# A routed expert kernel: four payload buffers, the last group's scatters among the tiles, and two thirds of the word loads on SyncE's queue

## The chip, the cores and the metric

The kernel runs on one core of a Trainium2 chip. The metric is device microseconds of one execution, and the median of the runs counts. A core has TensorE (PE), VectorE (DVE), ScalarE (ACT), GpSimd (POOL) and SyncE (SP); each works through its own instructions in order and waits on semaphores. SP, ACT and POOL also issue DMA transfers. In the profile an issue on SP or ACT stands as SPq or ACTq, a DMA issued by POOL as POOL.

## What is computed

There are 16 x 256 tokens of width 128 and 16 contexts of 64 keys.

```
x = x + attention(keys and values from ctx, queries from layernorm(x))
n = layernorm(x)
probs, idx = top_k(softmax(n @ Wr + br), 2)        # 8 experts, 2 for each token, probs normed to sum 1
h = layernorm(relu(n @ W1[e] + b1[e])) * g1[e] + be1[e]
y = layernorm(relu(h @ W2[e] + b2[e])) * g2[e] + be2[e]
x = x + sum over the 2 chosen experts of prob * y
```

Everything is float32. The kernel computes only the chosen experts' rows: 8192 token rows, sorted by expert into tiles of 128.

## The kernel before

**Group stage.** The 4096 tokens are 32 tiles in 8 groups of 4. For each group the kernel does attention, the second layernorm, the router and the choice of two experts. It counts, per expert, where each token's row goes (`pos`, a row number in the DRAM array `slot_rows`). A group's rows are put into a payload buffer `pay`: 128 high and 128 low halves in float16, then two words, the row number to which the answer must go, and the gate (L1202 `pay_hi` on ACT, L1556 `pay_lo` and L1741 `gate_rows` on DVE). There are two payload buffers, taken in turn; whoever writes a buffer waits until the eight scatters of the group two earlier have landed. SP copies the rows for the second choice (L533). POOL then sends eight indirect DMAs a group, one for each choice and tile (L659 `payload_out`), which scatter 128 rows each.

**Tile stage.** 71 tiles of 128 slot rows go through the experts. SP fetches a tile's rows transposed (L513 `tile_rows`, eleven buffers; it reads the row numbers from the table `row_tab` into registers, eight at a time). PE computes up and down products (`up`, `down_hi`, `down_lo`), ACT and DVE do ReLU, layernorms and the gate in a software pipeline: at position p ACT does the gate product of tile p-4 (L1378 `gate_share`, tile `rg`), which needs the two words of each row, and the final scaling (L1389, buffers `z`, five in turn). POOL loads the two words of every row of a tile (L686 `words`, `words_of`, 1 KB, twelve buffers) and scatters the finished rows into the DRAM array `answers` (L677 `answer`). In POOL's order, position p has the answer of tile p-4, then the words of tile p+2.

The first 24 tiles (`WHOLE`) hold only rows of the first four groups, so SP starts their transpositions during the last group; before tile 24, SP and POOL wait for all scatters. SP sends eleven transpositions, then the last group's payload copy, then eight stores of zero rows behind the experts' last rows (L571), then the other tiles. Of the last group's eight scatters POOL issues the first four ahead of the words and the other four at positions 2, 5, 8 and 11.

**End.** When the answers of a group are complete, SP fetches them (L551 `answers_back`, spread over the later tiles). PE adds the offset terms (L1071 `offset_sums`), DVE adds the two answers (L1957 `with_first`, L1967 `with_second`), ACT and SP store.

Of the kernel before, what the change touches and what calls it, by code (L numbers as in the profile page):

```python
# [23 lines left out]
def build(nc, A, out):  # L24
    P = 128
# [28 lines left out]
    ROW = 2 * D + 4  # L54
    MANTISSA, BIAS, LN2 = 23, 127, 0.6931471805599453
# [6 lines left out]
    with ctx:  # L62
# [125 lines left out]
        pos = sb("pos", [P, 2, K, GT], U32)  # L188
        pay = [sb(f"pay{n}", [P, K, GT, ROW], F16) for n in range(2)]
# [31 lines left out]
        NW, NS, LEAD = 12, 8, 2  # L221
# [122 lines left out]
        def as_row(ap, n):  # L344
# [3 lines left out]
        ld_wkq, ld_wv, ld_wo, ld_bq, ld_bvo, ld_br, ld_b1, ld_gb, ld_b2, ld_g2, ld_be2 = (  # L348
            signal("ld_" + n) for n in (
                "wkq", "wv", "wo", "bq", "bvo", "br", "b1", "gb", "b2", "g2", "be2"))  # L350
# [15 lines left out]
        p_setup, c_setup, c_exp, c_wrc, c_wkq, s_var1, s_guess1, s_sd, s_sel = (signal(n) for n in (  # L366
            "pe_setup", "act_setup", "exp_loaded", "wr_centred", "wkq_centred", "var1_eps", "rstd1_guess", "sd1",
# [8 lines left out]
        def ends(sem, order, step, done, ins):  # L376
# [12 lines left out]
        s_copy = [signal(f"pay_copy{n}") for n in range(2)]  # L389
        s_sc = [signal(f"scatter{n}") for n in range(2)]  # L390
# [6 lines left out]
        s_diag, s_share, p_share, s_shareT, p_off = (signal(n) for n in (  # L397
            "be2_diag", "shares", "pe_shares", "sharesT", "pe_offsets"))


        s_gm, s_ss, s_ss3, p_tot, s_tot, s_scale, s_w1x = (signal(n) for n in (
            "gains", "square_sums", "gain_square", "pe_totals", "totals", "scale", "w1_less_last"))
# [18 lines left out]
        s_word = [signal(f"words{n}") for n in range(NS)]  # L421
        s_backs = [signal(f"back{n}") for n in range(3)]
# [5 lines left out]
        def scattered(n):  # L428

            return 16 * K * GT * (n // 2 + 1)  # L430
# [39 lines left out]
        def sync(eng):  # L470
# [19 lines left out]
            eng.dma_start(b2row[:, :], flat("L0_ffn_b2").rearrange("(o n) -> o n", o=1)).then_inc(ld_b2, 16)  # L490
            eng.wait_ge(s_diag, 1)
# [19 lines left out]
            rows = []  # L511

            def tile_rows(j):  # L513
                if j >= NX:
                    eng.wait_ge(p_h, j - NX + 1)
                if j % E == 0:
                    half_regs = regs[j // E % 2 * E:(j // E % 2 + 1) * E]
                    table = row_tab[:, 0:WHOLE] if j < WHOLE else row_tab[:, :]
                    rows[:] = rows_of(half_regs, table, j, 0, E * REGION + (SPARE - 1) * P)
                here = bass.ds(rows[j % E], P)  # L520
                eng.dma_start_transpose(xsT[j % NX], slots[here, 0:2 * D]).then_inc(s_row[j % NX], 16)

            for g in range(GROUPS):
                if g == GROUPS - 1:
# [3 lines left out]
                    for n in range(2):  # L528
                        eng.wait_ge(s_sc[n], scattered(AHEAD - 2 + n))
# [3 lines left out]
                eng.dma_start(pay[g % 2][:, 1, :, 0:2 * D], pay[g % 2][:, 0, :, 0:2 * D]).then_inc(s_copy[g % 2], 16)  # L533
# [10 lines left out]
                for h in range(2):  # L544
# [4 lines left out]
                              ).then_inc(ld_g2, 16)  # L549
# [15 lines left out]
            for j in range(NX, SLOT_TILES):  # L565
# [6 lines left out]
                if j == WHOLE:  # L572
                    eng.wait_ge(s_zero, 16 * (E + 1))
                    for n in range(2):
                        eng.wait_ge(s_sc[n], scattered(GROUPS - 2 + n))
# [16 lines left out]
        def gpsimd(eng):  # L592
# [9 lines left out]
            eng.memset(be2_diag[:, :], 0.0).then_inc(s_diag, 1)  # L602
            eng.memset(zero_rows[:, :, :], 0.0).then_inc(s_zeros, 1)
            for n in range(2):
# [54 lines left out]
            def payload_out(g, k, i):  # L659
# [5 lines left out]
                if i == 0 and k == 1:  # L665
                    eng.wait_ge(s_copy[g % 2], 16 * (g // 2 + 1))
                eng.indirect_dma_start(  # L667
                    slot_words, bass.IndirectOffsetOnAxis(ap=pos[:, g % 2, k, i:i + 1], axis=0),
                    pay[g % 2][:, k, i, :].bitcast(U32), None).then_inc(s_sc[g % 2], 16)
# [16 lines left out]
            def words(j):  # L686

                if j == 0:
                    eng.wait_ge(s_tab, 1)
                    for n in range(2):  # L690
                        eng.wait_ge(s_sc[n], scattered(AHEAD - 2 + n))
                if j == WHOLE:
                    eng.wait_ge(s_tab, 2)
                    eng.wait_ge(s_zero, 16 * (E + 1))
                    for n in range(2):
                        eng.wait_ge(s_sc[n], scattered(GROUPS - 2 + n))
                if j % E == 0:
                    half_regs = regs[j // E % 2 * E:(j // E % 2 + 1) * E]
                    table = row_tab[0:1, 0:WHOLE] if j < WHOLE else row_tab[0:1, :]
# [17 lines left out]

        @block.tensor
        def tensor(eng):
# [131 lines left out]
            def gains():  # L851
                eng.wait_ge(ld_gb, 32)
# [4 lines left out]
            def totals():  # L857
                eng.wait_ge(s_ss, 2 * FC)
                eng.wait_ge(s_ss3, 1)
# [3 lines left out]
            def w_rows(h, part):  # L863

                first = h * H * FC
                if part == 0:
                    eng.wait_ge(ld_b2, 16)
# [53 lines left out]
            eng.wait_ge(c_wrc, 1)  # L921
            eng.wait_ge(ld_wo, 16)
            ends(p_setup, PE_SETUP, "wo", done, mm(bank[6][:, 0:D + E], WO, ident_wr[:, :]))
            eng.wait_ge(c_wkq, 1)
# [6 lines left out]
            eng.wait_ge(ld_wv, 16)  # L931
            mm(bank[7][:, 0:D + E], WV, woT[:, :])
            eng.wait_ge(ld_bvo, 32)
# [186 lines left out]
        def scalar(eng):  # L1120
# [81 lines left out]
            def pay_hi(g):  # L1202
                eng.wait_ge(s_xt, g + 1)
                if g >= 2:
                    eng.wait_ge(s_sc[g % 2], scattered(g - 2))
                if g == 0:
                    eng.wait_ge(s_const, 1)
                copy(pay[g % 2][:, 0, :, 0:D - 1], xt[:, :, 0:D - 1]).then_inc(s_hi, 1)
                copy(pay[g % 2][:, :, :, 2 * D:2 * D + 2].bitcast(U32)[:, :, :, 0],
# [21 lines left out]
            def c2_scaled():  # L1231
                eng.wait_ge(ld_off, 32)
# [23 lines left out]
            eng.dma_start(bcol[:, 1:2], A["L0_xattn_bv"].rearrange("(p o) -> p o", o=1)).then_inc(ld_bvo, 16)  # L1256
            eng.dma_start(bcol[:, 2:3], A["L0_xattn_bo"].rearrange("(p o) -> p o", o=1)).then_inc(ld_bvo, 16)
            eng.dma_start(brow[:, :], row1("L0_ffn_br").to_broadcast([P, E])).then_inc(ld_br, 16)
            eng.wait_ge(s_ones, 2)
            eng.activation(prob[0:1, 0, 0:1], ones[0:1, 0:1], ACT.Exp).then_inc(c_exp, 1)  # L1260
# [163 lines left out]
        def vector(eng):  # L1424
# [3 lines left out]
            def wkq_centred():  # L1428
# [3 lines left out]
                                         op0=ALU.mult, op1=ALU.add).then_inc(c_wrc, 1)  # L1432
# [123 lines left out]
            def pay_lo(g):  # L1556
                p = pay[g % 2]
# [37 lines left out]
            def pos_(g):  # L1595
                eng.wait_ge(q_pos, poss.n)
                if g >= 2:
                    eng.wait_ge(s_sc[g % 2], scattered(g - 2))
                with nc.allow_low_precision(reason="one whole number under 2 ** 24 among zeros"):
                    eng.tensor_reduce(pos[:, g % 2, :, :], pick[:, :, :].rearrange("p k (i e) -> p k i e", i=GT), AX.X,  # L1600
# [421 lines left out]
```

## Time and profile before

| | us |
|---|---|
| median of 3 runs | 272.37 |
| lowest and highest run | 269.18, 274.11 |
| profiled execution: span from first to last instruction | 268.4 |
| what lies around the span | not in the profile; the lowest run is 0.8 above the span, the median 4.0 |
| mean granted TensorE clock in the profiled execution | 0.955 |

The span is one execution; the run times are of others, so a sum made against the span is carried to the median by their difference. Times in rows are microseconds from the span's start. In a row of the timeline the first number is the start, the second the length; a group that is shown merged has its count at the end.

### The profile page before, as it was taken

To read this page: it belongs to the slowest core of one execution; us is meant where nothing else is said; L and a number is where in the kernel's file an instruction comes from. 1 tells how busy PE (TensorE), PEld (TensorE's weight loads), DVE (VectorE), ACT (ScalarE), POOL (GpSimd) and SP (SyncE) were. 2 spreads that over 40 slices of the span, in tenths; PEclk is the share of its full clock that TensorE was granted. 3 is DMA by queue.
4 is the path that set the end of the run, shared out by engine and by line. 5 is a ranking of instruction groups with operands and counts; after the bars stand their busy time and mean duration, and the time that the engine had idled before them with its cause. 6 is when DMAs were issued, how large, how long until landed. Compare 5 with 4: busy or idle time off the path is not lost.

```text
span 268.4 us, 10286 instructions
## 1 busy us (share of the span) xinstructions
PE 239.9 (89%) x2960; PEld 194.0 (72%) x2960; DVE 229.7 (86%) x1091; ACT 211.5 (79%) x795; POOL 190.6 (71%) x300
## 2 busy tenths in 40 slices
PE   1989779899888677679899999999999999999994
PEld 1564567777666434579899979999999999999330
DVE  0667986867689989689999988999999999999875
ACT  2465675789888888757999988999999999999700
POOL 8602277877757777775888888888888888878640
PEclk9997995899999759999999999999999999999999
DMA  6998398123425234354333443333315686772257
GB/s 159 313 299 295 91 271 279 51 89 92 139 82 136 83 91 99 84 119 94 84 90 67 89 82 81 73 72 75 84 33 142 155 155 141 149 143 86 68 187 233
DMA packets 48676, 34.56 MB, mean 129 GB/s; under 512 B 26871, under 2 KB 42743, under 8 KB 48620
## 3 DMA queue, kind: packets, MB, share of 16 engines
q1 hardware_dynamic: 38972, 22.80, 32.8%
q0 software_dynamic: 6592, 9.00, 12.7%
q10 hardware_dynamic: 3056, 2.11, 2.6%
q8 instruction: 25, 0.41, 0.7%
q14 instruction: 31, 0.25, 0.3%
HBM read 15.11 MB, written 12.02 MB: 101 GB/s over the span
## 4 chain that ended last, share of the span: by engine, by line
DVE 37%; issue 22%; PE 20%; ACT 9%; DMA 5%; DVEq 4%; SPq 1%; ACTq 0%
PE bank L721 15%; DVE vo L1873 8%; PE bank L725 4%; DMA w2f<-in_L_ffn_W 3%; DVE rs L1914 3%; DVE cx L1903 3%; DVE kq L1866 3%; DVE w2f L1653 3%; DVEq L1880 2%; DVE st L1891 2%; ACT ex L1175 2%; DVE mv L1897 1%; DMA wr<-in_L_ffn_Wr 1%; ACT xt L1198 1%; DVE topi L1573 1%
## 5 line engine op out<-in xcount | busy, mean ns | idle before, releaser
L679 POOL DMA_INDIRECT answers<-vo,words_of x71 | 70.6, 994 | 23.8 <-issue 19.4
L667 POOL DMA_INDIRECT slot_rows<-pay,pos x64 | 65.5, 1023 | 27.9 <-issue 18.5
L721 PE MATMUL bank<-kb_room,w1h 128*128 128x128 f16 x568 | 55.2, 219 | 1.7 <-issue 1.7
L725 PE MATMUL bank<-w2h,rh 128*128 x284 | 51.4, 219 | 1.6 <-ACT w2l L1122 1.6
L725 PE MATMUL bank<-rh 128*128 128x129 f16 x284 | 51.5, 220 | 0.0
L725 PE MATMUL bank<-w2l,rh 128*128 x284 | 51.4, 219 | 0.0
L721 PE MATMUL bank<-kb_room,w1l 128*128 128x128 f16 x284 | 51.2, 219 | 0.0
L1866 DVE SCALAR_TENSOR_TENSOR kq<-bank,rh 128x512 f16<-128x512 f32 x71 | 47.8, 673 | 0.1
L721 PEld LDWEIGHTS bank<-kb_room,w1h 128*128 x568 | 43.6, 98 | 2.6 <-issue 2.6
L1347 ACT ACTIVATE rh<-bank 128x512 f16<-128x512 f32 x71 | 41.1, 579 | 5.2 <-PE bank L721 4.2
L705 POOL DMA_DIRECT2D words_of<-slot_rows x71 | 40.8, 576 | 2.0 <-issue 1.8
L725 PE MATMUL bank<-w2h,kq 128*128 x284 | 40.3, 222 | 2.1 <-DVE kq L1866 1.7
L725 PE MATMUL bank<-rh,kq 128*128 128x129 f16 x284 | 39.8, 221 | 0.0
L1873 DVE CUSTOM_DVE_ANT_0 vo<-bank,square_mask 128x257 f32<-128x257 f32 x71 | 29.6, 418 | 2.2 <-issue 1.2
L725 PEld LDWEIGHTS bank<-w2h,kq 128*128 128x128 f16 x284 | 26.2, 97 | 6.6 <-DVE kq L1866 3.6
L725 PEld LDWEIGHTS bank<-w2h,rh 128*128 128x128 f16 x284 | 27.8, 98 | 3.4 <-ACT w2l L1122 1.8
L725 PEld LDWEIGHTS bank<-rh,kq 128*128 128x128 f16 x284 | 27.9, 98 | 0.0
L725 PEld LDWEIGHTS bank<-w2l,rh 128*128 128x128 f16 x284 | 27.8, 98 | 0.0
L721 PEld LDWEIGHTS bank<-kb_room,w1l 128*128 x284 | 27.8, 98 | 0.0
L725 PEld LDWEIGHTS bank<-rh 128*128 128x128 f16 x284 | 27.8, 98 | 0.0
L1389 ACT ACTIVATE vo<-cx,rg 128x128 f32<-128x128 f32 x71 | 27.5, 388 | 0.1
L1886 DVE SCALAR_TENSOR_TENSOR cxT<-bank,rs,c 128x128 f32<-128x128 f32 x71 | 24.9, 351 | 0.2
(259 smaller groups left out, 601.7 us busy)
## 6 DMA issues: line engine op xcount, KB each, us to landing
x_tok<-in_x SPq DMA_DIRECT2D x8, 256.0 KB, 7.7
w1f<-in_L_ffn_W SPq DMA_DIRECT2D x2, 1024.0 KB, 8.8
pay<-pay SPq DMA_DIRECT2D x8, 256.0 KB, 3.3
w1f<-answers SPq DMA_DIRECT2D x8, 256.0 KB
w2f<-answers SPq DMA_DIRECT2D x8, 256.0 KB, 2.9
kb_room<-slot_rows SPq DMA_TRANSPOSE x71, 3.3
words_of<-slot_rows POOLq DMA_DIRECT2D x71, 1.0 KB
answers<-vo,words_of POOLq DMA_INDIRECT x71
```

The source lines that it names most:

```text
L667: eng.indirect_dma_start(slot_words, bass.IndirectOffsetOnAxis(ap=pos[:, g % 2, k, i:i + 1], axis=0), pay[g % 2][:, k, i, :].bitcast(U32), ...
L679: eng.indirect_dma_start(answers, bass.IndirectOffsetOnAxis(ap=words_of[:, j % NW, 0:1], axis=0), z[j % NZ], None).then_inc(s_ans[j % NZ], 16)
L705: eng.dma_start(words_of[:, j % NW, :], slot_words[bass.ds(rows[j % E], P), D:]).then_inc(s_word[j % NS], 16)
L721: return eng.matmul(dst, lhsT, rhs, start=start, stop=stop)
L725: return eng.matmul(dst, lhsT, rhs, start=start, stop=False, skip_group_check=True)
L1347: eng.activation(rh_all(j), psH[j % 3][:, :].rearrange("p (c n) -> p c n", c=FC), ACT.Relu).then_inc(s_rh, 1)
L1389: eng.activation(z[j % NZ], w_[j % 3], ACT.Copy, scale=rg[j % 4][:, :]).then_inc(s_z, 1)
L1653: t = eng.scalar_tensor_tensor(out=w2f[:, n, :], in0=w2f[:, n, :], scalar=g1c[:, n:n + 1], in1=w2_mean[:, e_ * D:(e_ + 1) * D], op0=ALU.mu ...
L1866: eng.scalar_tensor_tensor(out=rl[j % 2][:, :, :], in0=psH[j % 3][:, :].rearrange("p (c n) -> p c n", c=FC), scalar=0.0, in1=rh_all(j), op ...
L1873: eng.tensor_tensor_reduce(squares[:, :], psY[j % 3][:, D:D + 2 * P + 1], square_mask[j % 2][:, :], 1.0, 0.0, ALU.mult, ALU.add, s2[j % 4] ...
L1886: eng.scalar_tensor_tensor(out=u[j % 3], in0=psY[j % 3][:, 0:D], scalar=rs1(j), in1=c2[:, bass.ds(off[j], D)], op0=ALU.mult, op1=ALU.add). ...
L1903: eng.scalar_tensor_tensor(out=w_[j % 3], in0=ur[j % 3], scalar=mv2[j % 4][:, 0:1], in1=g2[:, bass.ds(off[j], D)], op0=ALU.subtract, op1=A ...
```

## The change

The payload and position buffers are four instead of two, and a writer waits for the scatters of four groups earlier. All eight scatters of the last group go at the even positions 0 to 14 of POOL's tile order. Words of the tiles below `WHOLE`, and of odd tiles after it, are loaded by SP, each behind the transposition eight tiles ahead of it; POOL keeps the even tiles from 24. Besides, some setup semaphores are joined, the row of b2 is loaded earlier, and `b2row` and `w2_rows` share the room of other arrays.

```
+    NP = 4
...
-        b2row = sb("b2row", [1, E * D])
-        w2_rows = sb("w2_rows", [2, E * D])
+        b2row, w2_rows = w2_mean[0:1, :], c2[0:2, :]
...
-        pay = [sb(f"pay{n}", [P, K, GT, ROW], F16) for n in range(2)]
+        pos = sb("pos", [P, NP, K, GT], U32)
+        pay = [sb(f"pay{n}", [P, K, GT, ROW], F16) for n in range(NP)]
...
-        NW, NS, LEAD = 12, 8, 2
+        NW, NS, NSG, LEAD = 12, 8, 3, 2
+        WORDS_BEHIND = E
...
+        def words_by_sp(j):
+            return j < WHOLE or j % 2 == 1
+        def word_at(j):
+            return (j if j < WHOLE else WHOLE + (j - WHOLE) // 2) if words_by_sp(j) else (j - WHOLE) // 2
...
 SP:
+            eng.dma_start(b2row[:, :], flat("L0_ffn_b2").rearrange("(o n) -> o n", o=1)).then_inc(ld_gb, 16)
...
+            def words(j):
+                if words_by_sp(j):
+                    if j >= NW:
+                        eng.wait_ge(s_ans[(j - NW) % NZ], answered(j - NW))
+                    n = word_at(j)
+                    if n >= NS:
+                        eng.wait_ge(s_rg, tile_of_word(n - NS) + 1)
+                    eng.dma_start(words_of[:, j % NW, :], slot_words[bass.ds(place_of[j], P), D:]
+                                  ).then_inc(s_word[n % NS], 16)
...
                     for j in range(NX):
                         tile_rows(j)
+                        if j >= WORDS_BEHIND:
+                            words(j - WORDS_BEHIND)
...
                 tile_rows(j)
+                words(j - WORDS_BEHIND)
                 if j in back_at:
                     answers_back(back_at[j])
+            for j in range(SLOT_TILES - WORDS_BEHIND, SLOT_TILES):
+                words(j)
...
 POOL:
-            for g in range(GROUPS):
+            for g in range(GROUPS - 1):
                 for k in range(K):
                     for i in range(GT):
-                        if g < GROUPS - 1 or k == 0:
-                            payload_out(g, k, i)
+                        payload_out(g, k, i)
+            last_out = [(GROUPS - 1, k, i) for k in range(K) for i in range(GT)]
...
-                eng.dma_start(words_of[:, j % NW, :], slot_words[bass.ds(rows[j % E], P), D:]).then_inc(s_word[j % NS], 16)
-            for j in range(LEAD):
-                words(j)
+                n = word_at(j)
+                if n >= NSG:
+                    eng.wait_ge(s_rg, j - 2 * NSG + 1)
+                eng.dma_start(words_of[:, j % NW, :], slot_words[bass.ds(rows[j % E], P), D:]
+                              ).then_inc(s_word_even[n % NSG], 16)
             for p in range(SLOT_TILES + 4):
                 if 0 <= p - 4 < SLOT_TILES:
                     answer(p - 4)
-                if p + LEAD < SLOT_TILES:
+                if p + LEAD < SLOT_TILES and not words_by_sp(p + LEAD):
                     words(p + LEAD)
-                if p % 3 == 2 and p // 3 < GT:
-                    payload_out(GROUPS - 1, 1, p // 3)
+                if p % 2 == 0 and p // 2 < K * GT:
+                    payload_out(*last_out[p // 2])
...
 ACT:
-                eng.wait_ge(s_word[j % NS], 16 * (j // NS + 1))
+                eng.wait_ge(*word_landed(j))
```

## Rows read from the trace of the kernel before

**Rows 1.** The page's first part: busy us, share of the span, instructions.

```profile
PE 239.9 (89%) x2960; PEld 194.0 (72%) x2960; DVE 229.7 (86%) x1091; ACT 211.5 (79%) x795; POOL 190.6 (71%) x300
```

**Rows 2.** Stretch: length, busy PE, PEld, DVE, ACT, POOL, clock, DMA share, GB/s.

```profile
196.00:206.00 10.00, 10.00 (x175) 9.65 (x173) 10.00 (x45) 9.84 (x44) 8.18 (x12) 1.00 0.40 107
```

**Rows 3.** Timeline of VectorE (three sums of squares) and TensorE, tile stage.

```profile
118.76 0.42 DVE L1873 CUSTOM_DVE_ANT_0 vo<-bank,square_mask 128x257 f32<-128x257 f32 x1
...
179.96 0.42 DVE L1873 CUSTOM_DVE_ANT_0 vo<-bank,square_mask 128x257 f32<-128x257 f32 x1
181.81 0.42 DVE L1873 CUSTOM_DVE_ANT_0 vo<-bank,square_mask 128x257 f32<-128x257 f32 x1
...
113.48 0.22 PE L725 MATMUL bank<-w2h,rh 128*128 x1
115.28 0.22 PE L725 MATMUL bank<-w2h,rh 128*128 x1
```

**Rows 4.** Timeline of GpSimd; landing of its answers; ScalarE's products 10 and 13.

```profile
181.70 0.98 POOL L679 DMA_INDIRECT answers<-vo,words_of  x1 [0.30 <-issue]
182.68 0.57 POOL L705 DMA_DIRECT2D words_of<-slot_rows  x1
...
142.18 0.96 POOL L679 DMA_INDIRECT answers<-vo,words_of  x1 [0.30 <-issue]
...
DMA to landing us min/median/max: 2.8/2.9/3.3
...
142.43 0.40 ACT L1389 ACTIVATE vo<-cx,rg 128x128 f32<-128x128 f32 x1
148.06 0.39 ACT L1389 ACTIVATE vo<-cx,rg 128x128 f32<-128x128 f32 x1
```

**Rows 5.** The end: the chain of waits, then timelines of ACT, POOL and SP.

```profile
249.34 15.23 PE bank L721 x30
...
254.68 0.40 ACT L1389 ACTIVATE vo<-cx,rg 128x128 f32<-128x128 f32 x1
...
256.96 1.50 POOL L679 DMA_INDIRECT answers<-vo,words_of  x1 [0.30 <-issue]
...
260.56 0.90 SPq L557 DMA_DIRECT2D w2f<-answers  x2
```

**Rows 6.** Timeline of payload and scatter; landing of rows stored to and transposed from `slot_rows`.

```profile
104.03 0.63 ACT L1122 ACTIVATE pay<-xt 128x508 f16<-128x508 f32 x1
...
97.13 0.96 POOL L667 DMA_INDIRECT slot_rows<-pay,pos  x1 [0.30 <-issue]
...
DMA to landing us min/median/max: 2.7/3.3/4.8
```

**Rows 7.** Timeline of VectorE: the second part of the row table.

```profile
116.43 0.18 DVE L1700 SCALAR_TENSOR_TENSOR row_tab<-bank,slot_at 1x47 uint32<-1x47 f32 x1
```

**Rows 8.** Timeline of SP's queue: zero rows, then tiles 15, 16 and 23.

```profile
117.86 4.02 SPq L571 DMA_DIRECT2D slot_rows<-zero_rows  x8
...
128.80 1.17 SPq L521 DMA_TRANSPOSE kb_room<-slot_rows  x1
130.90 1.67 SPq L521 DMA_TRANSPOSE kb_room<-slot_rows  x1
...
141.56 1.18 SPq L521 DMA_TRANSPOSE kb_room<-slot_rows  x1
```

**Rows 9.** Timeline of ScalarE: the gate product of tile 16.

```profile
153.64 0.28 ACT L1382 ACTIVATE rg<-rs,words_of 128x1 f32<-128x1 f32 x1
```

**Rows 10.** Timeline of SP's queue: issues of small transfers.

```profile
67.49 0.33 SPq L539 DMA_DIRECT2D w_mean<-w_sums  x1
67.87 0.45 SPq L541 DMA_DIRECT2D c<-w_sums  x1
...
8.03 0.64 SPq L482 DMA_DIRECT2D gb<-in_L_ffn_g  x1
...
2.01 0.50 SPq L474 DMA_DIRECT2D bcol<-in_L_xattn_bq  x1
```

More of the change, by code:

```diff
@@ L388, in build @@
                 "rstd2_guess", "xt", "pay_hi", "pay_lo", "mask", "pe_rank", "pos", "pe_base"))
-        s_copy = [signal(f"pay_copy{n}") for n in range(2)]
-        s_sc = [signal(f"scatter{n}") for n in range(2)]
+        s_copy = [signal(f"pay_copy{n}") for n in range(NP)]
+        s_sc = [signal(f"scatter{n}") for n in range(NP)]
         q_stat, q_root1, q_root2, q_max, q_sum, q_top, q_pos, q_scale, q_tab, q_gate = (signal(n) for n in (
@@ L395, in build @@
         s_diff, s_gexp, s_gated, s_gate = (signal(n) for n in ("gate_diff", "gate_exp", "gates_in_rows", "gates"))
[L397 to L402, printed above, removed]
+        s_share, p_share, s_shareT, p_off = (signal(n) for n in (
+            "shares", "pe_shares", "sharesT", "pe_offsets"))
+        s_gm, s_ss, p_tot, s_tot, s_scale, s_w1x = (signal(n) for n in (
+            "gains", "square_sums", "pe_totals", "totals", "scale", "w1_less_last"))
         p_rows, s_rows_, st_sums, ld_off, s_c2, p_low, s_low = (signal(n) for n in (
@@ L421, in build @@
         s_word = [signal(f"words{n}") for n in range(NS)]
+        s_word_even = [signal(f"words_even{n}") for n in range(NSG)]
         s_backs = [signal(f"back{n}") for n in range(3)]
@@ L428, in scattered, with rows_out, tile_of_word, word_landed @@
         def scattered(n):
-            return 16 * K * GT * (n // 2 + 1)
+            return 16 * K * GT * (n // NP + 1)
+        def rows_out(eng, groups):
+            for g in range(max(groups - NP, 0), groups):
+                eng.wait_ge(s_sc[g % NP], scattered(g))
+        def words_by_sp(j):
+            return j < WHOLE or j % 2 == 1
+        def word_at(j):
+            return (j if j < WHOLE else WHOLE + (j - WHOLE) // 2) if words_by_sp(j) else (j - WHOLE) // 2
+        def tile_of_word(n):
+            return n if n < WHOLE else WHOLE + 2 * (n - WHOLE) + 1
+        def word_landed(j):
+            n = word_at(j)
+            return (s_word[n % NS], 16 * (n // NS + 1)) if words_by_sp(j) else (s_word_even[n % NSG], 16 * (n // NSG + 1))
         def answered(j):
@@ L510, in sync @@
             regs = [eng.alloc_register(f"row{n}") for n in range(2 * E)]
-            rows = []
+            place_of = {}
             def tile_rows(j):
@@ L518, in tile_rows @@
                     table = row_tab[:, 0:WHOLE] if j < WHOLE else row_tab[:, :]
-                    rows[:] = rows_of(half_regs, table, j, 0, E * REGION + (SPARE - 1) * P)
-                here = bass.ds(rows[j % E], P)
-                eng.dma_start_transpose(xsT[j % NX], slots[here, 0:2 * D]).then_inc(s_row[j % NX], 16)
+                    rows = rows_of(half_regs, table, j, 0, E * REGION + (SPARE - 1) * P)
+                    place_of.update({j + n: row for n, row in enumerate(rows)})
+                eng.dma_start_transpose(xsT[j % NX], slots[bass.ds(place_of[j], P), 0:2 * D]).then_inc(s_row[j % NX], 16)
+            def words(j):
[7 more added lines that the diff above has]
+                                  ).then_inc(s_word[n % NS], 16)
             for g in range(GROUPS):
@@ L573, in sync @@
                     eng.wait_ge(s_zero, 16 * (E + 1))
-                    for n in range(2):
-                        eng.wait_ge(s_sc[n], scattered(GROUPS - 2 + n))
+                    rows_out(eng, GROUPS)
                     eng.wait_ge(s_tab, 2)
                 tile_rows(j)
+                words(j - WORDS_BEHIND)
                 if j in back_at:
                     answers_back(back_at[j])
+            for j in range(SLOT_TILES - WORDS_BEHIND, SLOT_TILES):
+                words(j)
             for g in range(GROUPS - 2, GROUPS):
@@ L601, in gpsimd @@
                 eng.memset(second[:, n:n + 1], float(n))
-            eng.memset(be2_diag[:, :], 0.0).then_inc(s_diag, 1)
+            eng.memset(be2_diag[:, :], 0.0)
             eng.memset(zero_rows[:, :, :], 0.0).then_inc(s_zeros, 1)
-            for n in range(2):
+            for n in range(NP):
                 eng.memset(pay[n][:, 0, :, D - 1:D], 1.0)
@@ L686, in words @@
             def words(j):
[L688 to L691, printed above, removed]
                 if j == WHOLE:
@@ L694, in words @@
                     eng.wait_ge(s_zero, 16 * (E + 1))
-                    for n in range(2):
-                        eng.wait_ge(s_sc[n], scattered(GROUPS - 2 + n))
+                    rows_out(eng, GROUPS)
                 if j % E == 0:
                     half_regs = regs[j // E % 2 * E:(j // E % 2 + 1) * E]
-                    table = row_tab[0:1, 0:WHOLE] if j < WHOLE else row_tab[0:1, :]
+                    table = row_tab[0:1, :]
                     n = min(E, table.shape[1] - j)
@@ L1743, in gate_rows @@
                 tiles = slice(g * GT, (g + 1) * GT)
-                to = [pay[g % 2][:, k, :, 2 * D + 2:2 * D + 4].bitcast(F32)[:, :, 0] for k in range(K)]
+                to = [pay[g % NP][:, k, :, 2 * D + 2:2 * D + 4].bitcast(F32)[:, :, 0] for k in range(K)]
                 if k == 0:
```

71 lines of the change are left out of this document (33 added, 38 removed).

## The prediction, made before the changed kernel was run

> **What bounds the kernel now.** I read the page's line of busy time first [rows 1]: four engines stand between 71% and 89%, none is full, so an average decides nothing. The table by stretches shows what the average hides [rows 2]: in the tile stage, some 110 us of the span, VectorE is busy 10.00 of 10 us, TensorE too, ScalarE 9.84, GpSimd 8.18. Which of them paces it is seen in starts. VectorE's sum of squares comes every 1.85 us (179.96, 181.81). TensorE can do a tile in 1.80 us: 113.48 to 115.28, the same down-matmul of two tiles with nothing between them missing [rows 3]. GpSimd's answer of 0.98 us, its word load of 0.57 and the 0.30 that always passes before an answer make 1.85 to 1.86 us [rows 4]. So GpSimd looks like one more full engine. But nobody waits for it. A product may be written once the answer five tiles earlier has landed; the dearest case in this trace is answer 8, issued at 142.18 and landed 2.9 us later, at 145.1, for product 13 at 148.06 [rows 4]: 3 us of room. VectorE paces the stage.
>
> The end belongs to TensorE: in the chain of waits its offset sums run from 249.34 for 15.23 us, to 264.57, and VectorE's last additions and SP's stores follow. The last answer goes out at 256.96, SP fetches the last group at 260.56 [rows 5], and if that lands in the 2.9 us of an answer, both halves are there by 264, just before VectorE could use them.
>
> **The parts of the change.** *Four payload buffers.* They remove waits for the scatters of the group before last. The profile has no such wait: ScalarE writes the last group's payload at 104.03 with no idle time in front, and the last scatter from that buffer was issued at 97.13 and landed at most 4.8 us later, at 101.9 [rows 6]. The earlier groups have the same order of things, with 3 us and more of room. Worth 0. The added memsets lie in the first 10 us, where nothing waits for them.
>
> *Joined semaphores and shared rooms.* The setup's waits now take in a second or third transfer, all issued within a few issues of the first; the row of b2 ahead of W1 shifts W1 by one issue of about half a microsecond, and SP waits for W1 anyway. Worth 0; their cover is the slack of the setup.
>
> *GpSimd's load.* The row table is filled in parts of 24 and 47 tiles [rows 7], and the condition of the diff is that first part: SP takes words 0 to 23 and the 23 odd ones from 25 on, 47 in all. GpSimd sheds 47 x 0.57 = 27 us. In the tile stage that is worth nothing while VectorE needs 1.85 us. At the end the last product is ready at 254.68 plus 0.40, and its answer could start 0.30 later, at 255.4, instead of 256.96 [rows 5]; TensorE's 264.57 stays. Worth 0, covered by TensorE's offset sums.
>
> *The last group's scatters.* All eight now go at even positions, the last one behind answer 10. Product 10 ends at 142.43 plus 0.40 [rows 4], so that answer goes at 143.1, the scatter 1.3 us later, at 144.4, and it lands 3.3 us, at most 4.8 us, later [rows 6]: at 147.7, at most 149.2. SP before tile 24 and GpSimd before word 24 wait for it. Tile 24's rows are needed at position 22, two behind the gate product of tile 16 (153.64, [rows 9]), about 157.3; a transposition issued at 149.2 lands by 152.5 to 154.0. Worth 0.
>
> *SP's queue.* This step can cost. SP's transpositions take 1.17 us and come 1.52 us apart with their pauses (seven tiles from 130.90 to 141.56), 2.10 us where eight registers are loaded (128.80 to 130.90) [rows 8]. Now word j-8 is issued behind tile j. No row of before has a word load on SP. Its price is bounded by the nearest starts: below, 0.38 us, the step from 67.49 to 67.87 for a broadcast to 128 partitions; above, 0.69 us, the 0.64 of a load of 512-byte rows and the same 0.05 of hand-over [rows 10]. Nearest in shape are one element to each of 128 partitions, 0.50 plus 0.05 [rows 10], and the stores of 128 short rows at an address from a register, eight in 4.02 us, so (4.02 - 0.33) / 7 = 0.53 each [rows 8]. I take 0.53.
>
> Tile 23 is issued at 141.56 now [rows 8]. Fifteen words, those behind tiles 8 to 22, put it at 141.56 + 15 x 0.53 = 149.5. Its own word, 0.53, and the step with the register load, 2.10, put tile 24 at 152.1, later than the scatters' 149.2: SP's own order decides. Word 16 stands behind tile 24. A transposition lands 3.3 us after its issue [rows 6]; the word, issued at least 1.17 us behind it, I put at 3.5 us: 155.6. ScalarE wants word 16 at 153.64 [rows 9]. **2.0 us late.** Waiting there, the gate product holds up what stands behind it in ScalarE's order, the second ReLU, the scaled product and the standard deviation of the next tiles; VectorE's reciprocal waits for these, and TensorE for VectorE's reading of its banks. With VectorE full and TensorE's floor only 0.05 us lower, the 2.0 us are not won back. From word 24 on SP has only the odd ones: 1.52 + 0.27 = 1.79 us a tile, under 1.85, so it falls no further behind.
>
> The landing is where a page speaks. The Trainium skill (DMA: Bandwidth & Descriptors, Queues, rings and completion order) says that each DMA engine takes a ring's descriptors in order; by that a word cannot start before its transposition and would hardly land before the 3.3 us. Without such an order a small transfer's own landing might be a microsecond quicker, and the delay 1 us. No run so far shows a word behind a transposition.
>
> Sum: 268.4 (the span) + 0 + 0 + 0 + 0 + 2.0 = 270.4. The median of the three runs, 272.37, is 4.0 us above the profiled span, the lowest run 0.8 above. Carried to the median: **274.4 us**.
>
> **The rivals.** The lateness of word 16 is 141.56 + 15w + w + 2.10 + 3.5 - 153.64 = 16w - 6.5 for a word price w: nothing below 0.40 us, and 1.6 us for each 0.1 above.
>
> *Hidden anyway, 272.4 us.* At w = 0.38 word 16 is 0.4 us early. For it: some of SP's pauses (2.10 instead of 1.52) may take the words in. Against: the two nearest rows say 0.53 to 0.55.
>
> *GpSimd was dear, 269.2 us.* The runs go from 269.18 to 274.11. If late answers or scatters hold the products in the slower ones, the relief brings all to the lowest. For it: GpSimd's period is the longest of all. Against: 3 us of room in this trace. Another way to the same side is that VectorE's operations are stretched while GpSimd writes descriptors; relief would then stop at TensorE's floor, 71 x 0.05 = 3.6 us, 268.8. Against it: the sum of squares took 0.42 us at 118.76, when GpSimd was idle, and takes 0.42 us in the full stage [rows 3]. The Trainium skill (SBUF — State Buffer, Who interferes with whom) lets some VectorE operations and GpSimd shut each other out of a shared port; by that the gain would exist, and the equal lengths disagree with it.
>
> *SP becomes the pacer, 276.9 us.* At w = 0.69 the lateness is 4.5 us, at SP's queue between tiles 16 and 31, where every transposition has a word behind it. It passes 5.4 us at w = 0.75, or if SP's pauses grow with the longer program.
>
> **How the numbers follow.** SP's words late by 0.7 to 3.5 us (w from 0.45 to 0.62): 0.50, at 274.4. Hidden: 0.27, at 272.4. GpSimd dear: 0.12, at 269.2. SP the pacer: 0.11, at 276.9. Two per cent, 5.4 us, is about what a measurement can tell from no change. A gain of that size is beyond what TensorE's floor allows, but for luck in the runs: 0.03. A loss of that size is half of the last case and a tail of the first: 0.12. Within: 0.85. The range of 269.0 to 278.0 reaches from GpSimd's relief to the dear word and a little beyond; the likeliest case alone has 273.1 to 275.9.
>
> **What would show it.** In the trace after: a word load of about 0.53 us behind each of SP's transpositions from tile 8 to 31; tile 24 issued near 152; ScalarE's gate product idle for words first around tiles 9 to 17, and not for words 0 to 3; the last scatter near 144.4, with SP not held by it; GpSimd idle for products; VectorE's 1.85 us unchanged; TensorE's offset sums ending last. If SP's words take under 0.40 us, if VectorE's period moves, or if ScalarE nowhere waits for words, the forecast is wrong in that step.

## The result and the profile after

The changed kernel took **287.95 us** (median of 4 runs, 285.56 to 292.68) where the kernel before took 273.24 us on the same chip (4 runs, 269.18 to 275.53). The ratio is **1.060, 95% interval 1.046 to 1.073**: slower, where "within 2%" and 274.4 us had been forecast, and 10 us beyond the upper end of the range, 278.0. Some executions fall into a slower state, and the ratios leave these out, so they aren't the quotients of the medians. The profiled run took 287.46 us with a span of 285.8 us, 17.4 us over the span of before.

The busy line of the page, to be set beside [rows 1], says at once that the work is the same and only GpSimd's got less:

```profile
PE 242.0 (85%) x2960; PEld 193.8 (68%) x2960; DVE 231.2 (81%) x1091; ACT 212.2 (74%) x795; POOL 162.7 (57%) x257
```

GpSimd was relieved by 28 us (27 had been worked out), and each of the others does as many instructions in nearly the same time. So 17 us of idleness came in. The list of waits (engine, line, what was waited for: us in all, times, longest) names it:

```profile
POOL answers L717 <- ACT vo L1422: 62.7, 58, 11.2
...
ACT rg L1415 <- DMA words_of<-slot_rows: 18.2, 17, 3.2
DVE st L1923 <- ACT cxT L1403: 17.3, 17, 3.1
PE bank L760 <- DVE kq L1898: 16.7, 19, 3.1
```

Read the last three as one chain: ScalarE's gate product waits 18.2 us for words, VectorE 17.3 us for what stands behind it in ScalarE's order, TensorE 16.7 us for VectorE. No such wait for words is in the trace of before. The first line is a follower: GpSimd, with less to do, waits for products.

The same list for SP's queue has no line for a transposition or a word load. The waits that are left there are those of the setup, the group stage and the end; in the tile stage only two short ones are left, for a load of registers, 0.9 us in all. Before, SP waited 5.6 us in eleven places for buffers in front of transpositions, and 28.7 us in six places for answers, 13.9 of them in the tile stage. The line of before:

```profile
SPq L521 <- PE bank L721: 5.6, 11, 0.7
```

Accordingly the chain that ended last runs through SP's queue, first by engine, then by line (L545 is the transposition, L555 the word load, L593 the answers' fetch):

```profile
SPq 42%; PE 17%; DVE 14%; issue 9%; DMA 9%; ACT 6%; DVEq 1%; ACTq 0%
SPq L545 29%; PE bank L756 13%; SPq L555 6%; DMA words_of<-slot_rows 5%; DMA w2f<-in_L_ffn_W 3%; PE bank L760 3%; DVE w2f L1686 2%; ACT ex L1208 2%; SPq L531 2%; SPq L593 2%; SPq L607 2%; DMA wr<-in_L_ffn_Wr 1%; DVE kq L1898 1%; DVE topi L1606 1%; DVE w1f L1675 1%
```

SP's timeline shows what fills it; it answers to [rows 8]. Columns: start, duration, line, operation, tiles. An x2 (L593) is two issues in one row.

```profile
126.23 1.43 SPq L545 DMA_TRANSPOSE kb_room<-slot_rows  x1
127.86 0.44 SPq L555 DMA_DIRECT2D words_of<-slot_rows  x1
128.43 1.18 SPq L545 DMA_TRANSPOSE kb_room<-slot_rows  x1
129.80 0.43 SPq L555 DMA_DIRECT2D words_of<-slot_rows  x1
130.36 1.97 SPq L545 DMA_TRANSPOSE kb_room<-slot_rows  x1
...
154.13 0.37 SPq L555 DMA_DIRECT2D words_of<-slot_rows  x1
155.62 2.20 SPq L545 DMA_TRANSPOSE kb_room<-slot_rows  x1
158.11 0.34 SPq L555 DMA_DIRECT2D words_of<-slot_rows  x1
...
177.00 0.36 SPq L555 DMA_DIRECT2D words_of<-slot_rows  x1
...
213.03 1.17 SPq L545 DMA_TRANSPOSE kb_room<-slot_rows  x1
214.39 0.95 SPq L593 DMA_DIRECT2D w1f<-answers  x2
215.47 1.18 SPq L545 DMA_TRANSPOSE kb_room<-slot_rows  x1
216.91 1.03 SPq L555 DMA_DIRECT2D words_of<-slot_rows  x1
...
253.01 0.37 SPq L555 DMA_DIRECT2D words_of<-slot_rows  x1
```

From 126.23, tile 11, to 253.01, word 61, nothing but one issue after the other. A transposition follows another after 1.30 us. With a word between, 128.43 to 130.36, it is 1.93: a word costs 0.63 us, 0.37 to 0.43 of it its own length and the rest gaps around it. Ten times from 130.36 to 224.56, 6 to 16 us apart, an issue lasts 0.6 to 1.2 us longer than its kind: 1.97 at 130.36, 2.20 at 155.62 (tile 24), 1.79 at 164.90, 1.03 for the word at 216.91.

The gate product of tiles 3, 16, 25 and 61 in ScalarE's timeline (the first three lines of before, the last four of after; [rows 9] has tile 16 of before) dates the loss:

```profile
128.99 0.28 ACT L1382 ACTIVATE rg<-rs,words_of 128x1 f32<-128x1 f32 x1
...
172.34 0.28 ACT L1382 ACTIVATE rg<-rs,words_of 128x1 f32<-128x1 f32 x1
...
239.77 0.28 ACT L1382 ACTIVATE rg<-rs,words_of 128x1 f32<-128x1 f32 x1
```

```profile
130.42 0.29 ACT L1415 ACTIVATE rg<-rs,words_of 128x1 f32<-128x1 f32 x1 [1.35 <-DMA words_of<-slot_rows]
...
159.94 0.29 ACT L1415 ACTIVATE rg<-rs,words_of 128x1 f32<-128x1 f32 x1 [1.02 <-DMA words_of<-slot_rows]
...
179.60 0.28 ACT L1415 ACTIVATE rg<-rs,words_of 128x1 f32<-128x1 f32 x1
...
256.86 0.29 ACT L1415 ACTIVATE rg<-rs,words_of 128x1 f32<-128x1 f32 x1 [1.42 <-DMA words_of<-slot_rows]
```

Late by 1.4 us at tile 3, 6.3 at 16, **7.3 at 25 and 17.1 at 61**. The remaining nine tiles keep that distance, and the end looks as before, TensorE's offset sums of the chain of waits [rows 5] beginning 17.1 us later and the last answer 16.1 us later:

```profile
266.39 15.23 PE bank L756 x30
...
273.10 1.19 POOL L717 DMA_INDIRECT answers<-vo,words_of  x1 [0.30 <-issue]
```

### The profile page after: what moved, and what is told of

Read it like the earlier page. It is cut to its first block, busy times and chain, and to the rows that moved or that the text cites. A ratio compares the mean times of both kernels' runs of the same rounds, so it can differ in the third digit from the quotient of the medians.

```text
span 285.8 us, 10355 instructions
## 1 busy us (share of the span) xinstructions
PE 242.0 (85%) x2960; PEld 193.8 (68%) x2960; DVE 231.2 (81%) x1091; ACT 212.2 (74%) x795; POOL 162.7 (57%) x257
## 3 DMA queue, kind: packets, MB, share of 16 engines
q10 hardware_dynamic: 3056, 2.11, 2.5%
## 4 chain that ended last, share of the span: by engine, by line
SPq 42%; PE 17%; DVE 14%; issue 9%; DMA 9%; ACT 6%; DVEq 1%; ACTq 0%
SPq L545 29%; PE bank L756 13%; SPq L555 6%; DMA words_of<-slot_rows 5%; DMA w2f<-in_L_ffn_W 3%; PE bank L760 3%; DVE w2f L1686 2%; ACT ex L1208 2%; SPq L531 2%; SPq L593 2%; SPq L607 2%; DMA wr<-in_L_ffn_Wr 1%; DVE kq L1898 1%; DVE topi L1606 1%; DVE w1f L1675 1%
## 5 line engine op out<-in xcount | busy, mean ns | idle before, releaser
L717 POOL DMA_INDIRECT answers<-vo,words_of x71 | 69.1, 973 | 67.5 <-ACT vo L1422 62.7
L760 PE MATMUL bank<-w2h,kq 128*128 x284 | 40.4, 222 | 17.1 <-DVE kq L1898 16.7
L1923 DVE BATCH_NORM_STATS2 st<-cxT 128x6 f32<-128x128 f32 x71 | 20.5, 289 | 17.5 <-ACT cxT L1403 17.3
L1415 ACT ACTIVATE rg<-rs,words_of 128x1 f32<-128x1 f32 x71 | 20.3, 286 | 18.3 <-DMA words_of<-slot_rows 18.2
```

What stands on the lines that cost most here:

```text
L717: eng.indirect_dma_start(answers, bass.IndirectOffsetOnAxis(ap=words_of[:, j % NW, 0:1], axis=0), z[j % NZ], None).then_inc(s_ans[j % NZ], 16)
L760: return eng.matmul(dst, lhsT, rhs, start=start, stop=False, skip_group_check=True)
L1415: eng.activation(rg[j % 4][:, :], rs2(j), ACT.Copy, scale=words_of[:, j % NW, 1:2].bitcast(F32)).then_inc(s_rg, 1)
L1923: eng.bn_stats(st2[j % 4][:, :], ur[j % 3]).then_inc(s_st2, 1)
```

## The experiments

Theory A: SP's queue issues without a pause of its own from tile 11 on, and every issue on it counts in full. Rivals: a word on SP's queue lands late whatever stands ahead of it; the scatters and buffers are to blame; the order of word and transposition is.

**1. Which part: the words alone, the rest alone.** From the changed kernel, first the payload and the scatters were put back,

```
-    NP = 4
+    NP = 2
...
-            for g in range(GROUPS - 1):
+            for g in range(GROUPS):
...
+                        if g < GROUPS - 1 or k == 0:
+                            payload_out(g, k, i)
...
-                if p % 2 == 0 and p // 2 < K * GT:
-                    payload_out(*last_out[p // 2])
+                if p % 3 == 2 and p // 3 < GT:
+                    payload_out(GROUPS - 1, 1, p // 3)
```

then, with these as changed, only the words:

```
             def words_by_sp(j):
-                return j < WHOLE or j % 2 == 1
+                return False
```

> Only the words move to SP; two payload buffers and the last group's scatters as in the kernel before. Theory A (SP's queue is full from tile 11 to the end, because each word costs it about 0.6 us): all of the loss is here, ratio 1.06, some 16 us, ScalarE's gate product waiting about 18 us for words. Theory B (the payload buffers or the later scatters cost the time): ratio 1.00.

> Four payload buffers, all eight scatters of the last group among the tiles and the joined semaphores, but all words on GpSimd as in the kernel before. Theory A: ratio 1.00 within 0.01, SP's tile 24 held by the last scatter until about 148 to 150 without anyone waiting for it. Theory B: ratio 1.06.

Measured: words alone **288.63 us** (286.87 to 290.00), rest alone **274.69 us** (272.02 to 276.55), the kernel before 274.16 (269.17 to 277.21, 7 runs; it stands beside experiments 1 to 3). The words alone bring the whole loss. The gate product waits 12.8 us for words, where about 18 had been expected; between tile 0 and tile 70 it falls back by 15.5 us. SP goes from word 25 (176.97) to word 61 (253.02) in 76.0 us with two payload buffers as with four:

```profile
ACT rg L1416 <- DMA words_of<-slot_rows: 12.8, 15, 2.4
...
176.97 0.36 SPq L555 DMA_DIRECT2D words_of<-slot_rows  x1
...
253.02 0.37 SPq L555 DMA_DIRECT2D words_of<-slot_rows  x1
```

In the rest alone the later scatters do hold SP, once, for 11.2 us in front of tile 24. With all words on GpSimd an answer, a word load and every second time a scatter take it 5.0 us for two positions (the scatters at 138.83 and 143.82), where VectorE needs 3.7, so the last scatter goes at 153.79 and tile 24 at 157.59, later than the 148 to 150 expected. SP's lead is nearly long enough for that; TensorE waits about a microsecond for one transposition:

```profile
SPq L437 <- DMA slot_rows<-pay,pos: 11.2, 1, 11.2
...
PE bank L762 <- DMA kb_room<-slot_rows: 0.9, 1, 0.9
```

**2. Only the first 24 words.** The odd ones from 25 on go back to GpSimd.

```
-                return j < WHOLE or j % 2 == 1
+                return j < WHOLE
```

> SP loads only words 0 to 23, GpSimd all later ones. Theory A: SP is full up to tile 31 and then, with 1.55 us a tile against 1.85, recovers; the loss stops growing at word 23, where the changed kernel's gate product stood 7.3 us later than before (175.94 against 168.63): ratio 1.027. Theory C (a word on SP's queue is late because of its place behind a transposition, not because the queue is full): each late word costs alike, so half of the loss or more goes with the later words; the same ratio, but SP idle before some transpositions in tiles 11 to 31.

The counts of the semaphores follow, and GpSimd's own words; so it is in every experiment that changes who loads which word.

Measured: **280.02 us** (275.45 to 282.12), 5.9 us over the kernel before. In the profiled execution the gate product is already 4.9 us later than in that of before at tile 0, before ScalarE waited for any word; what counts is that it is 11.8 later at tile 61, 6.9 more. It waited in nine places, 7.1 us, last for word 23; then a tile takes 1.87 us, as before, and nothing more is lost. The words up to 23 make 6 to 7 us; the rest of the 17 comes from the odd ones, for which I had predicted no further loss.

```profile
ACT rg L1421 <- DMA words_of<-slot_rows: 7.1, 9, 1.6
...
180.63 0.30 ACT L1421 ACTIVATE rg<-rs,words_of 128x1 f32<-128x1 f32 x1 [0.58 <-DMA words_of<-slot_rows]
```

**3. Words four tiles earlier in SP's order.**

```
-        WORDS_BEHIND = E
+        WORDS_BEHIND = 4
```

> As the changed kernel, but word j-4 instead of j-8 stands behind tile j. Theory A: SP has the same work, only the words come four tiles, about 8.4 us, earlier in it; now the transpositions themselves are late (tile 70 was issued at 253.5 and is needed some 10 us before that plus its landing). Loss about 10 us, ratio 1.04. Theory C (the place alone): the words come in time and nothing is lost, ratio 1.00.

Measured: **286.44 us** (283.55 to 290.29), 1.5 us less than the changed kernel and within its spread. About 10 us over the kernel before had been expected, 12 came. No word is late any more, and now the transpositions are, 9.3 us in six places. ScalarE's wait of 20.1 us for TensorE has two parts, these waits and the granted clock: in three stretches, each just behind such a wait (they end at 162.48, 241.52 and 258.30), 163.5 to 170.5, 241.5 to 245.5 and 258.5 to 262.5, it is 0.54, 0.57 and 0.57 of full speed, which is the lower level, 1.2 GHz, for most of each.

```profile
ACT rh L1380 <- PE bank L756: 20.1, 12, 3.6
PEld bank L756 <- DMA kb_room<-slot_rows: 10.3, 6, 2.7
PE bank L756 <- DMA kb_room<-slot_rows: 9.3, 6, 2.5
```

A queue that is full is late in any order. It isn't the word's place or its landing.

**4. How many words, and where.** Words by SP: the odd ones from 25 on (23), or all odd ones (35).

```
-                return j < WHOLE or j % 2 == 1
+                return j >= WHOLE and j % 2 == 1      (23 words)
+                return j % 2 == 1                     (35 words)
```

> Words 0 to 23 are loaded by GpSimd's queue as in the kernel before, and SP loads only the odd words from 25 on (23 words); the rest is the changed kernel. Theory A (SP's queue is full: transposition 1.30 us, word 0.63 us, pauses, register loads and answer fetches, 2.11 us a tile measured after word 24 against VectorE's 1.85): SP stands some 9 to 10 us ahead of the gate product at tile 33 and loses 36 x (2.11 - 1.85) = 9 us of it by word 61, so the time comes out at 1.00 to 1.01 times the kernel before, with at most a few waits for words near the end. Rival B (every word on SP's queue lands late, whatever was ahead of it): half of the changed kernel's loss, 1.03. Rival C (GpSimd's work sets the time of the tiles): its 23 words fewer would make it about 0.98.

> SP loads the odd words of all 71 tiles (35), GpSimd's queue the even ones (36). Theory A: 1.88 us a tile up to tile 24 (1.30 + half a word of 0.63, pauses and register loads), so little of the lead is lost there but none is built up, then 2.11 us a tile to word 61, which is issued about 246.5 us into the span where the gate product of 61 stood at 239.8 in the kernel before: 8 us late with its landing, 1.03 times the kernel before, the waits of the gate product for words all behind tile 30. Theory B (lateness by word, whatever is ahead): 35/47 of the changed kernel's loss, 1.045.

Measured beside 273.41 us (269.10 to 276.30, 7 runs): 23 words **280.13 us**, ratio 1.035 (1.002 to 1.068); 35 words **280.18 us**, 1.032 (1.011 to 1.052).

All odd ones came out as theory A had it (1.03), though the interval doesn't exclude rival B's 1.045, and except that words were already waited for at tiles 17, 19 and 23 (2.1 us in all). Word 61 was issued at 248.92, where 246.5 was expected.

For the 23 words theory A's number, 1.00 to 1.01, lies at the lower edge of the interval, and the measured 1.035 is nearer to rival B's 1.03. The trace says why:

```profile
166.44 1.17 SPq L545 DMA_TRANSPOSE kb_room<-slot_rows  x1
167.81 0.43 SPq L555 DMA_DIRECT2D words_of<-slot_rows  x1
...
170.65 0.28 ACT L1421 ACTIVATE rg<-rs,words_of 128x1 f32<-128x1 f32 x1
...
204.53 0.96 SPq L593 DMA_DIRECT2D w1f<-answers  x2
...
207.04 0.37 SPq L555 DMA_DIRECT2D words_of<-slot_rows  x1
...
211.76 0.29 ACT L1421 ACTIVATE rg<-rs,words_of 128x1 f32<-128x1 f32 x1 [3.20 <-DMA words_of<-slot_rows]
```

Word 25 goes out at 167.81 and is wanted at 170.65. The words that ScalarE waited for in the changed kernel came 1.75 to 3.85 us after their issue (158.11 and 159.94 above are 1.83), so the lead was about 1 us by my estimate with 1.83, and less with a later landing, not the 9 to 10 I had taken. SP had been held before tile 24 by the scatters (11.2 us) and won back only 0.3 us a tile. Then it lost: words 25 to 61 took 167.81 to 244.35, 2.13 us a tile against VectorE's 1.86. (2.13 - 1.86) x 36 - 1 = 8.7 us of lateness; the gate product went from 1.7 us ahead of before at tile 25 to 6.8 behind at 61, 8.5, and the profiled span, 275.2, is 6.8 us over that of before.

The words 25 to 43 were all in time or 0.4 us late; the first long wait, 3.20 us, is for word 45, just behind a fetch of answers. It was issued 1.5 us before ScalarE was ready for it and landed 4.72 us after its issue; had it taken 1.83, the wait would be 0.3. So a word on SP's queue isn't late by being there (rival B); it is late when the lead is shorter than its landing, and the landings differ by 3 us, for a reason that no run here settles. Behind that wait TensorE's clock fell to the lower level (0.53 of full speed from 212.5 to 219.5; the columns are those of [rows 2]), and ScalarE waited 2.3 us for it; since word 61 was waited for again, the end was set by SP all the same.

```profile
212.50:219.50 7.00, 6.28 (x62) 6.28 (x63) 4.94 (x21) 4.60 (x20) 3.50 (x4) 0.53 0.47 131
```

Rival C falls too: with 23 of its word loads gone GpSimd left the sum of squares at 179.92 and 181.78, 1.86 us apart, as good as in [rows 3].

```profile
179.92 0.42 DVE L1911 CUSTOM_DVE_ANT_0 vo<-bank,square_mask 128x257 f32<-128x257 f32 x1
181.78 0.42 DVE L1911 CUSTOM_DVE_ANT_0 vo<-bank,square_mask 128x257 f32<-128x257 f32 x1
```

**5. The issue doubled, the bytes not.**

```
-                    eng.dma_start(words_of[:, j % NW, :], slot_words[bass.ds(place_of[j], P), D:]
-                                  ).then_inc(s_word[n % NS], 16)
+                    eng.dma_start(words_of[0:P // 2, j % NW, :], slot_words[...][0:P // 2, :]
+                                  ).then_inc(s_word[n % NS], 16)
+                    eng.dma_start(words_of[P // 2:, j % NW, :], slot_words[...][P // 2:, :]
+                                  ).then_inc(s_word[n % NS], 16)
```

> Each word of SP's queue is loaded by two DMAs of 64 rows in place of one of 128: the same bytes, the same places and waits, twice the issues. Theory A (the issues fill SP's queue): 47 further issues of 0.5 to 0.63 us, all on the path, so 24 to 30 us more than the changed kernel, 1.14 to 1.17 times the kernel before. Rival (the words are late by their transfer or landing, not by their issue): halves land no later than wholes, so no more than the changed kernel, 1.06.

Measured: **322.63 us** (315.46 to 323.04), 1.18 times the 273.41 of before, 35 us more than the changed kernel for 47 further issues.

```profile
ACT rg L1417 <- DMA words_of<-slot_rows: 41.8, 30, 4.3
...
223.61 0.47 SPq L555 DMA_DIRECT2D words_of<-slot_rows  x1
224.26 0.47 SPq L557 DMA_DIRECT2D words_of<-slot_rows  x1
224.87 3.51 SPq L545 DMA_TRANSPOSE kb_room<-slot_rows  x2
```

A half takes 0.47 us, more than the 0.37 of a whole, and its step is 0.65: the number of issues counts, not the bytes. Theory A's sum, with the step of a half 47 x 0.65 = 31 us, leaves out that the first half is longer than a whole, too. From one transposition to the next over a word it is 2.33 us in the mean in the changed kernel (38 steps) and 3.10 over two halves here (39 steps), 0.77 more; 47 of them are 36 us, where 35 were measured. The runs spread widely, though: between the shortest runs of both, 315.46 and 285.56, it is 30.

The Trainium skill (DMA: Bandwidth & Descriptors, Issuing engines are not separate DMA queues) says that spreading DMAs over several issuing engines saves only the sequencer's issue time, usually small beside the DMA itself. Small it is here as well, 0.63 us against 1.75 to 3.85 us to the landing, and yet it sets the time, on a queue that has no room.

**6. What else stands on the queue: the fetches moved to GpSimd.** In the changed kernel and in the one with 23 words, GpSimd issues the fetches of groups 0 to 5.

```
-                if j in back_at:
-                    answers_back(back_at[j])       (SP)
...
+            back_at = {}
+            for g in range(GROUPS - 2):
+                back_at[max(max(back_at, default=0) + 3, group_done(g) + 6)] = g
...
+                if p in back_at:
+                    answers_back(back_at[p])       (GpSimd)
```

> The changed kernel, but the twelve fetches of the first six groups' answers are issued by GpSimd's queue instead of SP's. Theory A (whatever SP issues after tile 11 sets the time, of whatever kind): the six pairs took 1.3 us each from SP's queue, all while it was full, so 8 us come back: about 1.03 times the kernel before. Rival (only the words' own landing is late): the fetches don't matter, 1.055 as the changed kernel. If GpSimd's queue, which waited 63 us for the products, can't take twelve issues more, its answers come late and the time is no better either.

> The same fetches on GpSimd's queue, in the kernel whose SP loads only the odd words from 25 on. That kernel came out 7 us over the kernel before, with 9 us of waits or delays behind word 45, where the fetches begin. Theory A: SP's pace falls from 2.11 to about 1.9 us a tile and the waits for words go, 1.00 to 1.01 times the kernel before. Rival (a word on SP's queue is late on its own): 1.03 as without the move.

These two met a chip on which the kernel before takes 326.49 us (324.98 to 329.31), so their times, 339.26 and 334.71 us, ratios 1.040 (1.032 to 1.048) and 1.025 (1.017 to 1.033), tell little on the question. They were run again beside the changed kernel itself:

> The changed kernel itself, beside the two below on one chip: the last two runs were on a chip on which the kernel before takes 326 us, so their times can't be set beside those of the others. If the chip is like the first, 1.06 times the kernel before (14 us more); theory A and the rivals say the same of it.

> The changed kernel with the answers' fetches of six groups on GpSimd's queue. Theory A: about 8 us (six pairs at 1.3 us of a full queue) under the run of the changed kernel in this call, that is 1.03. Rival (only the words' landing is late): no less than the changed kernel, 1.055 to 1.06.

> SP loads the odd words from 25 on, and the fetches are on GpSimd's queue. Theory A: 8 us of SP's queue less behind word 45 take away nearly all that this kernel's sister with the fetches on SP lost (7 us), 1.00 to 1.01; at most single waits for a word where a pause of SP falls on it. Rival (a word is late on its own): 1.03.

Measured beside 271.32 us (269.90 to 274.59, 7 runs): the changed kernel **288.26 us**, 1.051 (1.040 to 1.062); with the fetches moved **279.20 us**, 1.020 (1.009 to 1.031); 23 words and the fetches moved **274.48 us**, 1.012 (1.004 to 1.019). Moving twelve issues that have nothing to do with words brought 9.1 us (8.4 between the two shortest runs of each), 8 had been expected. From word 25 to word 61 SP now takes 68.6 us, 1.91 a tile, instead of 76.0:

```profile
174.21 0.36 SPq L555 DMA_DIRECT2D words_of<-slot_rows  x1
...
242.81 0.36 SPq L555 DMA_DIRECT2D words_of<-slot_rows  x1
...
ACT rg L1428 <- DMA words_of<-slot_rows: 9.0, 12, 1.8
```

With the 23 words five waits of 4.0 us in all are left. Its span is 3.4 us over that of the kernel before. Theory A's 1.00 to 1.01 reaches into its interval, the rival's 1.03 doesn't. Nothing that was run beats the kernel before, and nothing pointed to a version that would: the resource that was relieved isn't the one that sets the pace.

## Why the prediction was wrong

**The parts put at nothing held.** Buffers, joined semaphores and scatters together: 274.69 against 274.16. The runs of before on that chip go from 269.17 to 277.21, so a cost of 1 or 2 us wouldn't show; the traces bound it: the changed kernel's gate product of tile 0 comes 0.02 us after that of before, so setup and group stage cost nothing, and in the rest alone the tile stage loses 1.0 us. Within them one thing was off. The last scatter came at 148.38 instead of 144.4, since GpSimd waits for products that are late themselves; tile 24 was not held by it in the changed kernel, as forecast, but it is where SP carries no early words (11.2 us, hidden but for 1 in the rest alone; with the 23 words it ate the lead). GpSimd's relief is worth 0, as forecast: VectorE's step didn't move.

**The step that failed** is the sentence "From word 24 on SP has only the odd ones: 1.52 + 0.27 = 1.79 us a tile, under 1.85, so it falls no further behind." Measured from word 25 at 177.00 to word 61 at 253.01: 76.0 us for 36 tiles, **2.11 us a tile**, over VectorE's 1.85. Lateness went from 7.3 to 17.1 us there. Term by term, from the timeline:

- transpositions, 36 x 1.30 = 46.8 us, four register loads of about 0.9 = 3.6, and what is left over, 7.5, are issues that last longer than their kind (2.25 at 180.77, 1.57 at 195.54, 2.08 at 201.87, 1.91 at 210.06, 1.03 at 216.91 and others). Together 57.9, or 1.61 a tile; I had 1.52, from the seven tiles from 130.90 to 141.56. Two long issues are in it (1.67 at 130.90, 2.27 at 137.88), but no load of registers: +3.2 us, about the four loads
- 18 words at 0.63 = 11.3; I had 0.27 a tile, 9.7: +1.6 us
- six pairs of fetches of answers, 1.14 each = 6.8 us (213.03 to 215.47 is 2.44, a step of 1.30 is in it). **I had left them out altogether**: +6.8 us. In [rows 5] such a pair stands with 0.90 us, and before, nothing was queued behind it that anyone wanted soon.

Sum 11.6 us, which is 76.0 less my 36 x 1.79 = 64.4. Experiment 6 takes the third term away: SP's pace falls by 7.4 us over the stretch, the time by 9.1.

The trace of before was enough to see it. A pair of fetches stands there among transpositions, 1.08 us from its start to the next one:

```profile
213.30 0.96 SPq L557 DMA_DIRECT2D w1f<-answers  x2
214.38 1.20 SPq L521 DMA_TRANSPOSE kb_room<-slot_rows  x1
```

Six of them, and four register loads at the 2.10 - 1.52 = 0.58 us of [rows 8], are 8.8 us for 36 tiles: 1.79 + 0.24 = 2.03 us a tile, over 1.85 even with the word at 0.53. My own rule, that for a moved step each instruction on the queue that it is moved to has to be counted, was followed for transposition and word and not for the rest of that queue.

**The first stretch** was right in kind, too small in size. Tile 11 went at 126.23, where 123.6 follows from my 0.53 a word; tile 24 at 155.62 instead of 152.1; word 16 at 158.11, landed at 159.94, 6.3 us late instead of 2.0. A word at 0.63 instead of 0.53 is worth 16 x 0.1 = 1.6 us of it; most of the rest is long issues on a full queue, one of them among the zero rows (5.19 us for eight, 4.02 in [rows 8]), and 1.4 us were lost already at word 3, where I had expected no wait. The landing I had put at 3.5 us behind the transposition's issue; for word 16 it was 158.11 - 155.62 + 1.83 = 4.3, so 0.8 us of the error are there, and the 17 words that were waited for landed 3.2 to 5.3 us behind it.

**The rivals.** "SP becomes the pacer" was the right mechanism, with 0.11 and 276.9 us. I had bounded it to tiles 16 to 31, where each transposition has a word behind it, because the false 1.79 made the stretch after that safe; its own alarm, "or if SP's pauses grow", should have led me to ask what SP's rate is without any wait. "Hidden anyway" and "GpSimd was dear" are refuted by the first two experiments and by the sums of squares. That a sum of squares keeps its 0.42 us speaks for that operation alone; that VectorE's whole step stays at 1.86 us with 23 word loads off GpSimd is the better evidence. Of the things named in advance, GpSimd idle for products, VectorE's 1.85 and the end through TensorE's offset sums came as said; the word of 0.53 and "not for words 0 to 3" didn't.

## What to carry to other kernels

Before a step is moved to a queue, write down that queue's whole issue time per round of the loop, with every fetch, register load and long issue on it, and set it against the pace of the engine that leads: here 1.30 + 0.31 + 0.19 + 0.10 + 0.21 = 2.11 against 1.85 us, although SP looked idle. A relief is worth nothing on an engine that nobody waits for, and a lead is used up silently: the first late word says how far the lead reached, not where the cost lies. A deficit per tile is multiplied by all the tiles that follow, so the rate of the longest stretch deserves more care than the lateness at its beginning.

## What the runs showed of the hardware that was not expected

- SP's queue, full: a transposition every 1.30 us, a 1 KB load 0.63 us, a half of it 0.65, two fetches of 256 KB 1.14 us together. By itself an issue of 256 KB took 0.38 to 0.47 us (214.39 to 229.13), most of those of 1 KB 0.31 to 0.44.
- Every 6 to 16 us an issue on SP's queue took 0.6 to 1.2 us longer (130.36, 141.18, 155.62, 164.90, 180.77, 195.54, 201.87, 210.06, 216.91, 224.56), on a transposition or a word. The longer issues make a tenth of the stretch from word 25 to word 61. The trace of before has them too (2.27 at 137.88, 2.44 at 159.11). What they are wasn't settled.
- The 17 words that ScalarE waited for in the changed kernel reached it 1.75 to 3.85 us after their issue, 3.2 to 5.3 us after that of the transposition ahead; the longest landing in any other trace with whole words was 5.23 us after the issue. By the Trainium skill (DMA: Bandwidth & Descriptors, Queues, rings and completion order) each DMA engine takes a ring's descriptors in order, so a word's aren't taken before its transposition's. That no word came sooner than 3.2 us after the transposition's issue agrees with it, and doesn't prove it.
- TensorE's granted clock was 1.00 in the whole tile stage of the changed kernel (112 to 257), through idle times of 2.64 us before 221.96 and 3.08 before 249.45. With 23 words it fell to the lower level behind an idle time of 3.12 us before 213.22, and a matmul took 0.31 us instead of 0.22.
- One chip of those used took 326 us for the kernel for which the others took 271 to 274. The trace of the moved fetches there shows ScalarE idle in front of its first ReLU for something that the profile doesn't name, and VectorE waiting 32.1 us on ScalarE:

```profile
ACT rh L1393 <- remote: 28.7, 15, 2.7
```

Ratios from that chip are given with its own time of before; what slows it stays open.
